# A decoder layer with experts: the shared network in groups of four blocks, the experts unrolled, and a separate order for the last attention body

## The reference

```
x = layernorm(x + attn(x))     3 heads of width 512, mean over heads, then fc
x = layernorm(x + xattn(x, ctx))   16 heads of 32, causal, k and v from a latent of 128
logits = x @ gate_w.T ; scores = softmax(logits)          64 experts
topk_w, topk_idx = top_k(scores, 6)
per expert, for at most its first 128 rows:
    d = (silu(rows @ w_gate) * (rows @ w_up)) @ w_down     512 -> 352 -> 512
y = sum over the 6 of topk_w * d
y = y + (silu(x @ sh_gate.T) * (x @ sh_up.T)) @ sh_down.T  512 -> 704 -> 512, all rows
x = layernorm(x + y)
```

## Time and profile before

| | us |
|---|---|
| median of 3 runs (2252.64 to 2254.11) | 2253.65 |
| the profiled execution's own time | 2274.09 |
| its span, first to last instruction | 2272.3 |
| PE busy in the span | 2030.2 (89%) |
| DVE busy | 1682.4 (74%) |
| ACT busy | 1021.5 (45%) |
| POOL busy | 760.5 (33%) |
| mean granted clock of PE | 0.96 |

### The profile page before, as it was taken

The page is one execution under the profiler, slowest core; times in us unless marked ns, Lnnn a source line. Parts: engine busy times, 40 slices in busy tenths (PEclk is TensorE's granted clock), DMA queues, the critical chain, the costliest instruction groups (busy, mean ns, idle before and its releaser), DMA issues. The chain is left out here.

```text
span 2272.3 us, 50296 instructions
## 1 busy us (share of the span) xinstructions
PE 2030.2 (89%) x17648; PEld 1299.8 (57%) x17648; DVE 1682.4 (74%) x3743; ACT 1021.5 (45%) x1579; POOL 760.5 (33%) x631
## 2 busy tenths in 40 slices
PE   7989999999999999999999732999999999999960
PEld 3556666666656655666566521666666666666630
DVE  5457887888789778877887764667767767767758
ACT  4325453544344434534453423454554554544523
POOL 1011313431343134224422333344444444444420
PEclk9999999999999999999999865999999999999985
DMA  6831011001100110011010213778788778778746
GB/s 218 115 125 39 4 39 39 22 18 39 39 12 27 39 39 9 30 39 39 0 39 21 91 56 90 218 241 245 238 241 247 238 243 245 239 243 245 238 140 239
DMA packets 132885, 268.71 MB, mean 118 GB/s; under 512 B 32304, under 2 KB 42544, under 8 KB 132848
## 3 DMA queue, kind: packets, MB, share of 16 engines
q1 hardware_dynamic: 108176, 226.13, 30.9%
q0 software_dynamic: 20480, 33.71, 7.3%
q10 hardware_dynamic: 4192, 8.39, 1.0%
HBM read 217.12 MB, written 51.12 MB: 118 GB/s over the span
## 5 line engine op out<-in xcount | busy, mean ns | idle before, releaser
L680 POOL TENSOR_SCALAR_AFFINE_SELECT x_plus_shared<-x_plus_shared 128x1024 f32<-128x1024 f32 x64 | 70.7, 1104 | 743.5 <-ACT x_plus_shared L905 743.5
L705 PE MATMUL ring<-xT_split,tion_then_expert_weights 128*128 128x256 f16 x2304 | 267.6, 273 | 11.9 <-POOL xT_split L658 8.2
L705 PE MATMUL ring<-tion_then_expert_weights,xT_split 128*128 128x512 f16 x1152 | 259.5, 379 | 0.0
L107 POOL DMA_INDIRECT slot_table<-table_records,slot_of_choice x192 | 229.3, 1194 | 86.4 <-issue 56.5
L705 PEld LDWEIGHTS ring<-xT_split,tion_then_expert_weights 128*128 128x128 f16 x2304 | 220.6, 98 | 52.1 <-POOL xT_split L658 14.1
L889 ACT ACTIVATE x_plus_shared<-ring 128x512 f16<-128x512 f32 x224 | 130.7, 597 | 213.6 <-PE ring L705 210.6
L705 PEld LDWEIGHTS ring<-tion_then_expert_weights,xT_split 128*128 128x128 f16 x1152 | 109.0, 98 | 132.4 <-issue 7.9
L1005 DVE CUSTOM_DVE_ANT_0 quad<-quad,causal_penalty 128x128 f32<-128x128 f32 (+1 forms) x512 | 164.8, 394 | 15.4 <-PE quad L775 12.4
L966 DVE SCALAR_TENSOR_TENSOR x_plus_shared<-ring,x_plus_shared 128x512 f16<-128x512 f32 x192 | 130.3, 685 | 55.4 <-ACT x_plus_shared L889 55.3
L1248 POOL DMA_INDIRECT expert_sums<-tion_then_expert_weights,scatter_index x64 | 149.8, 2341 | 59.0 <-POOL scatter_index L1245 55.7
L1245 POOL COPY scatter_index<-records 128x1 uint32 (+1 forms) x64 | 39.8, 622 | 315.8 <-DMA expert_sums<-tion_then_expert_weights,scatter_index 158.3
(11 more groups left out here) (199 smaller groups left out, 4104.4 us busy)
## 6 DMA issues: line engine op xcount, KB each, us to landing
tion_then_expert_weights<-in_w_gate SPq DMA_DIRECT2D x64, 704.0 KB
tion_then_expert_weights<-in_w_up SPq DMA_DIRECT2D x64, 704.0 KB
tion_then_expert_weights<-in_w_down SPq DMA_DIRECT2D x64, 512.0 KB, 3.9
tion_then_expert_weights<-in_w_down SPq DMA_DIRECT2D x64, 192.0 KB, 4.1
xT_in<-in_xT SPq DMA_DIRECT2D x16, 512.0 KB, 4.6
x_in<-in_x SPq DMA_DIRECT2D x16, 512.0 KB, 5.0
expert_sums<-zero_rows SPq DMA_DIRECT2D x16, 512.0 KB, 11.5
x_rows<-x_plus_shared SPq DMA_DIRECT2D x16, 512.0 KB, 2.8
```

What stands on the lines that cost most here:

```text
L107: pool.indirect_dma_start(self.dram, bass.IndirectOffsetOnAxis(ap=self.slot[:, tb, c:c + 1], axis=0), self.record[:, tb, c, :], None, boun ...
L680: pool.affine_select(out=p32[:, g % 2, :, 0:2 * P], in_=p32[:, g % 2, :, 0:2 * P], compare_op=ALU.is_ge, fill=0.0, base=0, pattern=[[0, 4] ...
L705: last = pe.matmul(out_, left(a, c), right(b, c), start=(n == 0), stop=(n == 3 * chunks - 1))
```

## The change

What it does, stage by stage:

- `prepare`: the first two matrices come in eight chunks of 256 KB, and the first fold's four banks are filled chunk by chunk. All M folds come before all A folds.
- `attend`: the zero stores of body 0 go. Instead every body stores x2 to `expert_sums` too, so that the residual is in it from the start. Body 16 follows lists of its own (`PE_LAST` and so on), with NX1, T and Q ahead of NX2 and TX, and RM and RS late on DVE. SP loads the first four blocks of x2's transpose in body 17.
- `experts`: no loop; one list `MOE` of 694 steps, made by `all_jobs`. The shared network works on groups of four blocks with its weights stationary and x2's transpose moving, 512 columns (four blocks) at a time; its hidden values come out transposed and need no SHT. Of 704 hidden rows five pieces of 128 have an SG and an SU; the last 64 rows of both share one product, SP. SH is the split of a piece (ACT and DVE). SD has 17 matmuls a block. Its result is scaled by DVE to `sd32`, and POOL adds two blocks at a time to `expert_sums`, 512 KB, in the same chain of adds as the experts' (80 adds in all).
- The first group and the start of the second (11 SG, SU or SP products, then four more and one SD) stand ahead of the first X. After that shared jobs are spread among the experts' jobs in proportion to PE columns. The shared weights are split in pieces (WS), and expert weights have three float32 slots.
- `finish`: no addition of z.

```diff
+    items, slots = [], []
+    for d in range(EC):
+        items.append((rows(fcT)[:, d:d + 1, :], lambda k, d=d: fs[:, k, d:d + 1, :], E))
+        items.append((rows(wv[0])[:, d:d + 1, :], lambda k, d=d: vs[:, k, 0, d:d + 1, :], E))
+        slots += [(0, d * E), (1, d * E)]
+    CHUNKS = len(items)
+    for h in range(1, H):
+        items.append((rows(wv[h]), lambda k, h=h: vs[:, k, h, :, :], EC * E))
...
-    folds = [(kind, h, c) for h in range(H) for kind in ("M", "A") for c in range(EC)]
+    slots += [(n % NSTAGE, 0) for n in range(2, len(items) - CHUNKS + 2)]
+    folds = [(kind, h, c) for kind in ("M", "A") for h in range(H) for c in range(EC)]
     def operands_split(kind, h):
-        return 2 + 3 * h if kind == "M" else 4 + 3 * h
-    staged = [mem.sem(f"staged{k}") for k in range(NSTAGE)]
+        return CHUNKS + (h if kind == "M" else H - 1 + 2 * (h + 1))
...
+            for d in range(EC):
+                pe.wait_ge(low, 2 * (d + 1))
+                for c in range(EC):
+                    for n, (a, b) in enumerate(PASSES):
+                        last = pe.matmul(bank[c][:, :], vs[:, a, 0, d, c * P:(c + 1) * P], fs[:, b, d, :],
+                                         start=(d == 0 and n == 0), stop=(d == EC - 1 and n == 2))
+                    if d == EC - 1:
+                        last.then_inc(folded, 1)
...
+PE_LAST = [
+    ("C", 0, 0), ("K", 0, 0), ("K", 1, 0), ("T", 0, 0), ("T", 1, 0), ("Q", 0, 0), ("Q", 1, 0), ("TX", 0, 0),
+    ("TX", 1, 0), ("M", 0, 0), ("M", 1, 0), ("R", 0, 0), ("M", 2, 0), ("M", 3, 0), ("C", 1, 0), ("MT", 0, 0),
+    ("MT", 1, 0), ("ST", 0, 0), ("ST", 1, 0), ("CT", 0, 0), ("ST", 2, 0), ("AV", 0, 0), ("ST", 3, 0),
+    ("AV", 1, 0), ("AV", 2, 0), ("AV", 3, 0), ("OUT", 0, 0), ("OUT", 1, 0),
...
+DVE_LAST = [
+    ("K", 0, 0), ("C", 0, 0), ("T", 0, 0), ("T", 1, 0), ("K", 1, 0), ("Q", 0, 0), ("Q", 1, 0), ("TX", 0, 0),
+    ("M", 0, 0), ("TX", 1, 0), ("M", 1, 0), ("M", 2, 0), ("M", 3, 0), ("MT", 0, 0), ("MT", 1, 0), ("R", 0, 0),
+    ("RC", 0, 0), ("C", 1, 0), ("CT", 0, 0), ("P", 0, 0), ("P", 1, 0), ("AV", 0, 0), ("AV", 1, 0),
+    ("P", 2, 0), ("OM", 0, 0), ("P", 3, 0), ("AV", 2, 0), ("OM", 1, 0), ("AV", 3, 0), ("OM", 2, 0),
+    ("OM", 3, 0), ("RM", 0, 0), ("RS", 0, 0), ("OUT", 0, 0), ("OUT", 1, 0), ("LN", 0, 0),
...
-                for r in range(0, T, 2 * P):
-                    sp.dma_start(moe_d[r:r + 2 * P, :].rearrange("(p r) n -> p (r n)", r=2), w["zeros"][:, :])\
-                      .then_inc(filled, 16)
-                    n += 1
...
-                    sp.dma_start(x2_d[bass.ds((i - 2) * N, N), :].rearrange("(t p) e -> p t e", p=P),
-                                 x2[:, :, :]).then_inc(x2_stored, 16)
+                    for d in (x2_d, moe_d):
+                        sp.dma_start(d[bass.ds((i - 2) * N, N), :].rearrange("(t p) e -> p t e", p=P),
+                                     x2[:, :, :]).then_inc(x2_stored, 16)
...
-MOE = [
-    ("WG", 0), ("WU", 0), ("SG", 0), ("SU", 0), ("WG", 1), ("SG", 1), ("X", 0), ("SU", 1), ("WU", 1),
-    ("X", 1), ("G", 0), ("SHT", 0), ("SHT", 1), ("U", 0), ("WD", 0), ("G", 1), ("HT", 0), ("U", 1),
-    ("D", 0), ("HT", 1), ("WD", 1), ("SD", 0), ("D", 1),
-]
...
+def shared_jobs():
+    jobs = []
+    for g in range(GROUPS):
+        for j in range(SC6 - 1):
+            late = [("SH", g, j - 1)] if j else [("SH", g - 1, SC6 - 1)] if g else []
+            jobs.append([("SG", g, j)] + late + [("SU", g, j)])
+            if g and j < GROUP:
+                jobs.append([("SD", g - 1, j)])
+        jobs.append([("SP", g, SC6 - 1), ("SH", g, SC6 - 2)])
+    jobs[0:2] = [[("SG", 0, 0), ("SG", 0, 1)], [("SU", 0, 0)], [("SH", 0, 0), ("SU", 0, 1)]]
+    return jobs + [[("SH", GROUPS - 1, SC6 - 1), ("SD", GROUPS - 1, b)] if b == 0 else [("SD", GROUPS - 1, b)]
+                   for b in range(GROUP)]
+def expert_jobs():
+    jobs = [[("X", 0)], [("X", 1)]]
+    for e in range(NX + 1):
+        if e < NX:
+            jobs.append([("G", e)] + ([("WG", e + 1)] if e + 1 < NX else []))
+        if e > 0:
+            jobs.append([("HT", e - 1)] + ([("WD", e)] if e < NX else []))
+        if e < NX:
+            jobs.append([("U", e)] + ([("WU", e + 1)] if e + 1 < NX else []))
+        if 0 < e < NX - 1:
+            jobs.append([("X", e + 1)])
+        if e > 0:
+            jobs.append([("D", e - 1)])
+    return jobs
+COLUMNS = dict(SG=12 * 512, SU=12 * 512, SP=12 * 512, SD=17 * 512, G=12 * F, U=12 * F, D=9 * 512, X=4 * 340, HT=3 * 340)
+def all_jobs():
+    first = [("WS", "SG", c) for c in range(EC)] + [("WS", "SU", c) for c in range(EC)]
+    down = [("WS", "SD", c) for c in range(SC6)] + [("WG", 0), ("WU", 0), ("WD", 0)]
+    shared, own = shared_jobs(), expert_jobs()
+    def columns(job):
+        return sum(COLUMNS.get(step[0], 0) for step in job)
+    order = list(first)
+    for n, job in enumerate(shared[:BEFORE_EXPERTS]):
+        order += job
+        if n >= 2:
+            order += down[:2]
+            down = down[2:]
+    order += own.pop(0) + own.pop(0) + shared[BEFORE_EXPERTS]
+    left = shared[BEFORE_EXPERTS + 1:]
+    all_left, all_own = sum(map(columns, left)), sum(map(columns, own))
+    done = done_left = 0
+    for job in own:
+        order += job
+        done += columns(job)
+        while left and (done_left + columns(left[0]) / 2) * all_own < done * all_left:
+            done_left += columns(left[0])
+            order += left.pop(0)
+    assert not left and not down
+    return order
...
+            for step in MOE:
+                if step in MOE_WEIGHTS and step[1] + 3 < NX:
+                    name, e = step
+                    sp.wait_ge(w_low, MOE_WEIGHTS[step])
+                    if name == "WD":
+                        loads.down(sp, e + 3)
+                    else:
+                        loads.projection(sp, name, e + 3)
+                elif step[0] == "SP" and step[2] == SC6 - 1 and step[1] + 2 < GROUPS:
+                    sp.wait_ge(full, MOE_JOBS[step])
+                    loads.blocks(sp, x2T_d, step[1] + 2)
...
+            def add_expert(e):
+                s = e % 2
+                n = MOE_ADDS["D", e]
+                if e >= 2:
+                    pool.wait_ge(added, 16 * MOE_ADDS["D", e - 2])
+                pool.wait_ge(free, MOE_FREED["D", e])
+                index(si[:, s, :], e)
+                if n > 1:
+                    pool.wait_ge(added, 16 * (n - 1))
+                own_wait(pool, taken)
+                pool.indirect_dma_start(moe_d, bass.IndirectOffsetOnAxis(ap=si[:, s, :], axis=0),
+                                        d32[:, s, :], None, bounds_check=T + CAP - 1,
+                                        compute_op=ALU.add).then_inc(added, 16)
+            def add_shared(g, b):
+                n = MOE_ADDS["SD", g, b]
+                t = GROUP * g + b - 1
+                pool.wait_ge(free, MOE_FREED["SD", g, b])
+                if n > 1:
+                    pool.wait_ge(added, 16 * (n - 1))
+                own_wait(pool, taken)
+                pool.dma_start(moe_d[t * P:(t + 2) * P, :].rearrange("(t p) n -> p t n", p=P),
+                               sd32[:, b - 1:b + 1, :], accum_op=ALU.add).then_inc(added, 16)
...
+            for step in MOE:
+                if step[0] == "X" and step[1] + 2 < NX:
+                    gather(step[1] + 2)
+                elif step[0] == "D":
+                    add_expert(step[1])
+                elif step in MOE_ADDS:
+                    add_shared(step[1], step[2])
...
+            def shared_columns(step):
+                name, g, j = step
+                col = j * P if name != "SU" else FS + FC_ROWS + j * P
+                name_at = {("SG", 0, 0): "SG", ("SU", 0, 0): "SU"}.get(step)
+                return product(bank_of(step)[:, :].rearrange("p (b n) -> p b n", b=GROUP),
+                               lambda a, c: gu[:, a, c, col:col + P],
+                               lambda b, c: x2t[:, g % 2, :, b, c, :], EC,
...
+                    for f in range(SC6 - 1):
+                        for a, b in PASSES:
+                            pe.matmul(o[:, :], hs[:, s, a, f, b0:b0 + P], sd[:, b, f, :], start=(k == 0), stop=False)
+                            k += 1
+                    pe.matmul(o[:, :], hs[:, s, 0, SC6 - 1, b0:b0 + P], sd[:, 0, SC6 - 1, :], start=False, stop=False)
+                    last = pe.matmul(o[:, :], hs[:, s, 0, SC6 - 1, b0:b0 + P], sd[:, 1, SC6 - 1, :],
+                                     start=False, stop=True)
...
+                elif step in MOE_SPLITS:
+                    act.wait_ge(full, MOE_JOBS[step])
+                    cols, half = halves(step)
+                    act.activation(half(0), bank_of(step)[:, 0:cols], ACT.Copy).then_inc(high, 1)
+                elif step in MOE_WEIGHTS:
+                    act.wait_ge(w_in[name, e % 3], (16 * (e // 3) + 16) * (2 if name == "WD" else 1))
+                    if e >= 2:
```

(28 more changed lines are left out.)

574 lines of the change are left out of this document (281 added, 293 removed), and 4 rows, old and new, of the table ACT_LAST.

## The result

The changed kernel takes 2280.83 us (median of 4 runs, 2276.95 to 2285.28), the kernel before 2253.14 (4 runs, 2251.50 to 2254.11): a ratio of 1.0124, 95% interval 1.0107 to 1.0141, 27.7 us slower. The forecast was 2274.

What follows compares the result with a forecast made beforehand. PE was taken as the bound in attention and most expert bodies, paid per column, with DVE's chain setting the last stage's end. Terms summed to +20 us on the 2253.65 median: 2274 us, range 2195 to 2325.

Steps and rivals of the forecast that it cites:

- The new order of the experts: Expert stage: G and D wait for DVE's splits in the new list, +88 us (bounds 50 and 110).
- -22 for the first body: First expert body: shared products ahead of the first X hide the gather, -22 us (bounds 0, -27).
- The shared network: Shared network's PE work: SHT transposes go and SD has 17 matmuls for 18, -28 us.
- The chain of adds: POOL's expert and shared adds, each waiting for all before it: fits barely in the expert stage, +3 us.
- The end: Last matmul to last stage's loads: final adds end later, and last HT to D has nothing between, +15 us.
- Preparing: Start of the kernel: smaller first weight chunks let PE start near 6.5 us, -7 us (bounds 0 and -8).
- the last stage: Final stage: six adds of 18.0 us leave DVE's chain, some tiles arrive late, -15 us (bounds 0, -18).
- attention: Attention bodies: no zero stores, body 1 gets input earlier, second store per body hidden, -1 us (bounds -3, +2).
- The last body: Last attention body: NX1 first, RM, CT and RS behind P and AV, -10 us (bounds 0, -20).
- the hand-over: Attention to experts: splits in pieces let SG start after one small ACT and DVE pass, -3 us.
- DVE's chain would be hidden: Rival, expert stage: late D and G are not seen, so the 88 us go; 2228 or 2180, chance 0.30.
- the adds pace: Rival, expert stage: at 18 us per shared add the adds set the pace, +36, 2307 us; chance 0.13.

Runs made afterwards that it cites:

- The two edits: Changed kernel with shared jobs listed only behind an X: 2198.48 us; separately, changed kernel with X right behind G and DVE's WD split behind D: 2223.11 us.
- three buffers: Kernel with X behind G, shared jobs only behind HT and SH(7,5) earlier, given three gathered-row buffers for two: 2194.46 us, ratio 0.9646 to before.

## Why the prediction was right, and where it was not

**The new order of the experts**, the largest term, was sized at +88; the waits shown above are 79.7 (58.3 for gathered_T_split, 21.4 for hidden_T_split, of which the last D has 1.3). By kind: 15 stretches with the shared job ahead of HT wait 2.45 to 2.59 us (2.6 predicted for 15), 13 D's 1.45 to 1.59 (1.6 for 12), 9 SD's between HT and X 0.9 to 1.1 (1.2 to 1.3 for 10), SG and SU there 0.3 to 0.7 (0.7 for 10); the last two were a little too large. The two edits that took the waits away by order alone show the cause: +88 was not a property of the work but of the list.

**What the term left out** are three costs, together 29 us, and they are why the experts cost +57.3 and not +42:
- PE's clock. Behind seven of the gaps the granted clock falls from 1.00 to 0.50 (2.4 to 1.2 GHz): behind the 6.6 us ahead of SD(7,0), and behind six of the 17 gaps of 2.45 to 3.1 us ahead of a G. That costs 13.2 us, each job's time against its time at the full clock (11.2 behind the six, 2.0 in SD(7,0)). In the changed kernel the stretches of 2 us around the gap of 3.10 us at 1467.9 to 1471.0 read:

```profile
1466.00:1468.00 2.00, 1.89 (x9) 0.68 (x7) 1.84 (x3) 1.28 (x3) 0.97 (x2) 1.00 0.96 306
1468.00:1470.00 2.00, 0.00 (x0) 0.00 (x0) 1.81 (x3) 0.00 (x0) 1.50 (x1) 1.00 0.99 334
1470.00:1472.00 2.00, 1.02 (x5) 0.65 (x6) 1.46 (x3) 0.00 (x0) 0.18 (x1) 0.82 0.94 275
1472.00:1474.00 2.00, 2.00 (x9) 1.01 (x7) 0.00 (x0) 0.00 (x0) 1.25 (x1) 0.50 0.97 365
```

 G takes 3.2 us there, not 1.8. In the stage without gaps (three buffers) the mean clock is 1.00.
- SD(7,0) behind SH(7,5), 6.6 us. The list shows it: SH(7,5) stands right ahead of SD(7,0). I had counted stretches from G to G and never asked what SD waits for.
- The end of the last matmul before each gap, some 0.16 us (a D takes 1.94 us from start to start in a full stream, its row lasts 2.11 where PE then stands), 55 times, some 9 us.

By the prediction's terms: -22 for the first body is borne out (27.0 us were idle or cold in it; at the start 2.5 us cold and 2.1 at G1 and the first SD are left). The shared network gives -31 for -28: 780 us of matmuls in the 807.2 of before, 749 now, each job at its time from start to start at the full clock; the stage without gaps, 752.5 us busy, holds 2.3 us cold besides. The chain of adds costs 0 where 3 was said.

**The end** was the other wrong size: +4.8 where +14 was forecast, since a shared add was taken at 13 and an expert's at 8.9. The six adds from D60's on take 40.8 us (2187.72 to 2228.47) and not 55. With nothing else moving (POOL's last three adds in the changed kernel):

```profile
2208.72 1.57 POOL L1367 DMA_INDIRECT expert_sums<-tion_then_expert_weights,scatter_index  x1 [0.89 <-POOL scatter_index L1340]
2214.19 1.27 POOL L1379 DMA_DIRECT2D expert_sums<-tion_then_expert_weights  x1 [3.90 <-DMA expert_sums<-tion_then_expert_weights,scatter_index]
...
2220.82 1.66 POOL L1367 DMA_INDIRECT expert_sums<-tion_then_expert_weights,scatter_index  x1 [5.15 <-DMA expert_sums<-tion_then_expert_weights]
```

5.5 us from the expert's add to the next issue, 6.6 from the shared one's (5.15 of it idle), and the loads follow at 2228.47; in the expert stages of the kernels here a shared add took 6.5 to 12.5 where the next one waited for it. The Trainium skill (DMA: Bandwidth & Descriptors, Anatomy of one DMA) would give the shared add 3.2 us: no add here is that fast, and the 8.9 us of the earlier trace rows is the loaded case, which the end is not.

**Preparing** (-8.2 for -7), **the last stage** (-17.8 for -15, DVE busy 34.9 us as said; it idles 14.9 us there and idled 14.7 before, so loads and stores at 337 GB/s did not hold it) and **attention** (0 for -1) stand. **The last body** gave 6.5 for 10, and the hand-over, by what is left, 3.6 for 3. The 29 us that the order's term left out, the 3.5 of the body and the 1 of attention are set off by 9 too many in the order's waits, 9 at the end, 3 for the adds, 3 for the shared network and some 4 for preparing and the last stage. So the total is right to 6 us of span (7.7 by the medians) with a term 29 us short. The direction and the wait behind it were foreseen; that the number came out so near is luck.

**The rivals.** That DVE's chain would be hidden is refuted by the 7.15 us read above and by 82 us from an edit of the list alone. That the adds pace is refuted for this change by the run without the shared ones.

## What to carry to other kernels

Write down, for each product, the last step of every other engine that it waits for, and what stands ahead of that step in the same engine's list: work that nobody waits for soon (here the splits of weights that arrive three experts ahead) belongs behind it, and long independent jobs belong into the gap between. An order in which a busy engine showed no gap is worth as much as the work that a change saves; here 53 us of saving in the same stage were bought with 109 of waits and of what followed from them. Count waits by every kind of step, also the one-off ones, and add the clock and the drain to each gap; then go on to the queue that is next, here POOL's.
